# Constants of a 256-step recurrence: from bf16 matmuls to copies into PSUM by ScalarE

## The reference

```
# layer 0: gated recurrence; xz, xr, xh = x @ W_z, W_r, W for all steps; v* = cond @ C* + b*
z = sigmoid(xz[t] + h @ U_z + vz)
r = sigmoid(xr[t] + h @ U_r + vr)
hh = tanh(xh[t] + (r * h) @ U + vh)
h = (1 - z) * h + z * hh
# layer 1: h starts as cond, leak = 1 - alpha
gate = sigmoid(h1 @ Wh.T + x1[t] @ Wz.T + b)
h1 = tanh(h1 * leak + gate * x1[t])
# layer 2: forget and input gates, cumulative products and sums over the steps, started from cond
# layer 3: c = layernorm(cond); hid = gelu(c @ W1 + bias1); w = hid @ W2 + bias2  -> rank 8 factors
#          mid = gelu(x @ base_down + ranks); out = mid @ base_up + ranks
```

## Time and profile before

| | us |
|---|---|
| median of 3 runs (1059.47 to 1060.64) | 1059.53 |
| profiled execution | 1062.49 |
| its span | 1060.7 |

### The profile page before, as it was taken

How to read it: one execution, slowest core, us unless ns; L and a number is a source line. 1 busy time by engine, 2 the same in 40 slices (tenths; PEclk the granted TensorE clock), 3 DMA queues, 4 the chain that set the end, 5 groups by cost and what they waited for, 6 DMA issues and landing times.

```text
span 1060.7 us, 121712 instructions
## 1 busy us (share of the span) xinstructions
PE 988.8 (93%) x55016; PEld 831.4 (78%) x55016; DVE 764.0 (72%) x2501; ACT 507.9 (48%) x2279; POOL 258.3 (24%) x654
## 2 busy tenths in 40 slices
PE   3599999999999999999999999969999999999987
PEld 2599999999999999999999999426566665665655
DVE  2166666666666666666666666699999999999993
ACT  2155555555555555555555555324444444434440
POOL 0022222222222222222222222322322322222220
PEclk9699999999999999999999999989999999999998
DMA  4113303311010010010010010100000100001001
GB/s 168 70 45 112 104 22 114 101 27 30 22 35 22 25 32 22 25 32 25 22 35 22 22 35 22 40 0 23 23 22 22 45 22 22 22 22 40 27 23 40
DMA packets 38292, 42.00 MB, mean 40 GB/s; under 512 B 5120, under 2 KB 31232, under 8 KB 37120
## 3 DMA queue, kind: packets, MB, share of 16 engines
q1 hardware_dynamic: 37408, 41.24, 12.4%
q10 hardware_dynamic: 864, 0.49, 0.2%
HBM read 32.80 MB, written 8.91 MB: 39 GB/s over the span
## 4 chain that ended last, share of the span: by engine, by line
PE 60%; DVE 29%; issue 8%; ACT 1%; DVEq 1%; DMA 1%; ACTq 0%
PE bank L651 31%; PE bank L669 22%; DVE arena L578 10%; DVE wx L590 4%; DVE cx L594 4%; PE bank L661 3%; DVE cx L603 2%; DVE cx L607 2%; DVE wx L576 2%; DVE cx L599 2%; DVE y L618 2%; PE bank L800 1%; PE bank L817 1%; DVE none_h L518 1%; DMA bias<-in_bias 1%
## 5 line engine op out<-in xcount | busy, mean ns | idle before, releaser
L669 PE MATMUL bank<-x_ahead,wx 128*32 128x64 f32 x12384 | 298.6, 222 | 3.3 <-issue 3.3
L661 PE MATMUL bank<-ident,const_stack 96*32 96x64 bf16 x4144 | 251.0, 197 | 6.2 <-issue 4.5
L651 PE MATMUL bank<-none_h,urz 128*32 128x32 f32 x16384 | 215.2, 201 | 20.5 <-DVE none_h L518 13.9
L669 PEld LDWEIGHTS bank<-x_ahead,wx 128*32 128x32 f32 x12384 | 223.9, 111 | 3.7 <-issue 3.7
L651 PEld LDWEIGHTS bank<-none_h,urz 128*32 128x32 f32 x16384 | 188.7, 111 | 33.5 <-DVE none_h L518 27.0
L273 POOL TENSOR_TENSOR leaked<-leak,h_f 128x64 f32<-128x64 f32 x256 | 83.0, 324 | 501.0 <-ACT h_f L366 501.0
L506 DVE TENSOR_TENSOR rh_f<-r_f,none_h 128x32 f32<-128x32 f32 x512 | 104.5, 244 | 136.4 <-ACT r_f L346 136.4
L800 PE MATMUL bank<-x,wl 128*128 (+1 forms) x384 | 179.0, 605 | 0.9 <-DVE rank_rows L555 0.9
L518 DVE TENSOR_TENSOR_SCAN none_h<-zero_z,cand_kept 128x64 f32<-128x64 f32 x512 | 121.5, 279 | 79.8 <-ACT cand_kept L355 79.8
L661 PEld LDWEIGHTS bank<-ident,const_stack 96*32 96x32 bf16 x4144 | 143.3, 97 | 7.0 <-issue 5.2
L366 ACT ACTIVATE h_f<-pre 128x64 f32<-128x64 f32 x256 | 65.9, 257 | 164.0 <-DVE pre L540 164.0
(11 more groups left out here) (81 smaller groups left out, 1387.7 us busy)
## 6 DMA issues: line engine op xcount, KB each, us to landing
x_in<-in_x SPq DMA_DIRECT2D x34, 256.0 KB, 2.7
x_ahead<-in_x SPq DMA_DIRECT2D x130, 64.0 KB, 1.8
arena<-in_w SPq DMA_DIRECT2D x8, 1024.0 KB, 5.5
out<-y SPq DMA_DIRECT2D x32, 256.0 KB, 2.4
rank_rows<-in_bias_rows SPq DMA_DIRECT2D x1, 1024.0 KB, 5.0
arena<-scratch SPq DMA_DIRECT2D x64, 16.0 KB
cx<-in_cx SPq DMA_DIRECT2D x1, 768.0 KB, 4.5
wx<-in_wx SPq DMA_DIRECT2D x1, 768.0 KB, 7.4
```

The lines of the kernel that those rows point to most:

```text
L651: mm = pe.matmul(out(m)[32 * j:32 * j + 32], weights(k, j, m), moving(k), start=False, stop=k == 1, tile_position=(0, 32 * j), skip_group_ ...
L661: pe.matmul(out[32 * j:32 * j + 32], const_stack[:, j, gate * SLAB + m * BLK:gate * SLAB + (m + 1) * BLK], ident[:].rearrange("p v b -> p ...
L669: pe.matmul(out[32 * j:32 * j + 32], weights(k, j, m), moving(k), start=False, stop=False, tile_position=(0, 32 * j), skip_group_check=True)
```

## The change

- ACT copies the constants (as 128x128 float32 pieces, `seed_rh`, `seed_z`, `seed_g`) into the PSUM banks ahead of each block, and the matmuls of `constants` are gone. Two copies stand behind the candidate of each odd step (reset and candidate banks), two behind that of each even step (update bank, layer 1 bank). PE waits for `rh_seeded`, `z_seeded` and `g_seeded`.
- In the opening matmuls with zeros set the banks' state once; the constants are computed transposed, straight in feature order; the bf16 parts, the identity and their stacks are gone. Loads are reordered and spread over SyncE's and ACT's queues.
- The waits at three places are written in the other order.
- SyncE's load of a block's x waits for one count of `r_pre` less (`2 * ((c - 2) * STEPS) + 1` for `2 * (c * STEPS - 3)`; a step gives two counts).
- The adapter's gelu moves from the opening on ACT to behind `second_state` of step 3. Behind the loop the adapter's products and the last two layer 1 gates stand in another order.

```diff
@@ scalar
+            act.wait_ge(bits_set, 1)
+            act.wait_ge(seeds_ready, 8)
+            seed_reset(0)
+            seed_keep(0)
+            seed_reset(1)
+            seed_gate(1)
             act.wait_ge(ln_step, 3)
             act.activation(std[:], var_eps[:], ACT.Sqrt).then_inc(std_done, 1)
-            act.wait_ge(hid_pre, 1)
-            for m in range(HALVES):
-                act.activation(hid_f[:, m], banks[4][:, m * B:(m + 1) * B], ACT.Gelu,
-                               bias=bias1[:, m:m + 1]).then_inc(hid_done, 1)
...
+            def hidden():
+                act.wait_ge(hid_copied, 1)
+                for m in range(HALVES):
+                    act.activation(hid_f[:, m], hid_raw[:, m], ACT.Gelu, bias=bias1[:, m:m + 1]).then_inc(hid_done, 1)
...
                     candidate(n, u)
+                    t = n * BODY + u
+                    if u % STEPS:
+                        seed_reset((u // STEPS) % 2, 2 * t + 2)
+                    else:
+                        if second or u:
+                            act.wait_ge(z_done, 2 * t)
+                        seed_keep(1 - (u // STEPS) % 2)
+                        if second:
+                            act.wait_ge(gate_done, t - LAG + 1)
+                        else:
+                            act.wait_ge(gate_pre, u + 1)
+                        seed_gate(((u - LAG) // STEPS) % 2)
                     if second:
                         second_state(n, u)
+                    if first and u == LAG:
+                        hidden()
@@ vector
                 for m in range(HALVES):
-                    dve.wait_ge(cand_done, 2 * t + m + 2)
                     if m == 0:
                         dve.wait_ge(kept_done, t + 1)
+                    dve.wait_ge(cand_done, 2 * t + m + 2)
@@ tensor
-            def ahead(out, gate, m, weights, moving, start):
-
-                constants(out, gate, m, start)
+            def ahead(out, m, weights, moving):
+
                 for k in range(HALVES):
...
+            def ahead_first(block, par, gate, m):
+
+                if gate == 0:
+                    pe.wait_ge(rh_seeded, 2 * block + m + 1)
+                elif gate == 1 and m == 0:
+                    pe.wait_ge(z_seeded, block + 1)
...
                 def state_ready(k):
-                    pe.wait_ge(h_done, 2 * t + k + 1)
                     if k == 0:
                         pe.wait_ge(cand_done, 2 * t + 1)
+                    pe.wait_ge(h_done, 2 * t + k + 1)
...
                 def reset_ready(k):
-                    pe.wait_ge(rh_done, 2 * t + k + 1)
                     if k == 0:
                         pe.wait_ge(r_done, 2 * t + 2)
+                    pe.wait_ge(rh_done, 2 * t + k + 1)
```

More of the change, by code:

```diff
@@ L198, in next_turn @@
                 for c in range(2, BLOCKS + 2):
-                    sp.wait_ge(r_pre, 2 * (n * BODY + c * STEPS - 3))
+                    sp.wait_ge(r_pre, 2 * (n * BODY + (c - 2) * STEPS) + 1)
                     sp.dma_start(x_ahead[:, c % 2], io["x"][:, bass.ds(n * BODY + c * STEPS, STEPS)]
@@ L451, in _, with repeated, seed @@
         def _(dve):
+            dve.memset(zero_z[:], 0.0).then_inc(zero_done, 1)
+            dve.memset(cand_kept[:], 0.0).then_inc(cand_done, 1)
+            dve.memset(none_h[:, 1], 0.0).then_inc(h_done, 2)
+            dve.memset(x1_f[:], 0.0).then_inc(x1_done, 1)
+            dve.memset(h1_f[:, 0], 0.0)
+            dve.wait_ge(alpha_in, 32)
+            dve.memset(eps[:], EPS).then_inc(eps_done, 1)
+            dve.tensor_scalar(leak[:], leak[:], -1.0, 1.0, ALU.mult, ALU.add).then_inc(leak_done, 1)
+            dve.transpose(bias_f[:].rearrange("p a m b -> p (a m b)"),
+                          bias_rows[:].rearrange("p a e -> p (a e)")).then_inc(bias_done, 1)
+            dve.wait_ge(bias_done, 1)
+            def repeated(out, *parts):
+                return [bass.broadcast_tensor_aps(out, part)[1] for part in parts]
+            for m in range(HALVES):
+                dve.tensor_copy(seed_g[:, m], *repeated(seed_g[:, m], bias_f[:, 3, m:m + 1])).then_inc(seeds_ready, 1)
+            dve.wait_ge(first_in, 16 * len(FIRST_LOADS))
+            dve.wait_ge(const_pre, 1)
+            def seed(out, gate, m):
+                const, bias = repeated(out, pre_const[:, gate, m:m + 1], bias_f[:, gate, m:m + 1])
+                dve.tensor_tensor(out, const, bias, ALU.add).then_inc(seeds_ready, 1)
+            for m in range(HALVES):
+                seed(seed_rh[:, m, 0], 0, m)
+                seed(seed_rh[:, m, 1], 2, m)
+            for m in range(HALVES):
+                seed(seed_z[:, m], 1, m)
             dve.wait_ge(adapter_in, 16 * len(ADAPTER_LOADS))
@@ L493, in _ @@
[L493 to L500 removed]
+            dve.wait_ge(hidden_in, 16 * len(HIDDEN_LOADS))
@@ L656, in recur @@
                 return mm
-            def constants(out, gate, m, start):
-                for j in range(SLABS):
-                    pe.matmul(out[32 * j:32 * j + 32], const_stack[:, j, gate * SLAB + m * BLK:gate * SLAB + (m + 1) * BLK],
-                              ident[:].rearrange("p v b -> p (v b)"), start=start, stop=False,
-                              tile_position=(0, 32 * j), skip_group_check=True)
-            def ahead(out, gate, m, weights, moving, start):
-                constants(out, gate, m, start)
+            def ahead(out, m, weights, moving):
                 for k in range(HALVES):
@@ L746, in second_gate @@
                       lambda k: h1_f[:, (s - 1) % 2, k]).then_inc(gate_pre, 1)
-            for par in range(2):
-                for m in range(HALVES):
-                    constants(pre_g[par][:, m].rearrange("p v b -> p (v b)"), 3, m, start=m == 0)
             FILL = [[(0, 0)], [(0, 1)], [(2, 0)], [(2, 1), (1, 0), (1, 1)]]
```

171 lines of the change are left out of this document (78 added, 93 removed).

## The result

| | before | after |
|---|---|---|
| median of 5 runs each, us | 1060.16 (1059.47 to 1060.64) | 1064.09 (1062.78 to 1066.27) |
| ratio to before, 95% interval | | 1.0042 [1.0026, 1.0059] |
| profiled execution, its span | 1062.49, 1060.7 | 1062.78, 1060.9 |
| four steps in the middle, us | 9.76 | 9.90 |

The change makes the kernel slower by 0.4%. The forecast was 1051. The two profiled executions lie closer together than the medians, because that of before is above its median and that of after is the fastest of its five: 0.3 us apart, the medians 3.9. The difference of 3.6 us is spread between runs.

What follows compares the result with a forecast made beforehand. It took three steps of four to be bound by the cycle PE, ACT, DVE, PE, and one by PE. Terms -6.3, -3.3, +2.9, +1.0, -3.0 and +0.3 sum to -8.4: median 1051.1 us, own range 1045 to 1057, with rivals 1039 to 1059.

Steps and rivals of the forecast that it cites:

- part 5: 60 turns in the loops: constants, PE's and DVE's waits, copies and load sum to -0.05 a turn, -3.0 us.
- Part 1: Opening up to the first product with the state: splitting of constants goes, loop starts at 17.4 for 23.75, -6.3 us.
- Part 2: PE's first turn: fewer matmuls, about one idle piece in seven has nothing to bring in, -3.3 us.
- Parts 3 and 4: Ahead of step 4: gelu's table loads hold up the reset gate, +2.9 us; clock may return late, +1 us.
- Constants: Loop turn: constant matmuls taken off PE, a set taking 0.03; -0.09 ahead of the branch, -0.06 ahead of U's product.
- PE's wait: Loop, three steps of four: the state's wait on a separate instruction delays PE's weights; +0.05 a step, +0.15 a turn.
- Less 0.01 for new register instructions: Loop, ahead of the product with U: new register instructions reduce the constants' gain from -0.06 to -0.05 a turn.
- Part 6: Steps 4 to 15: the scan's well-placed candidate wait is lost, +0.10 in each of three turns, +0.3 us.
- C: Rival: ACT's copies end late and hold up h_f and r_f, +51 us over 256 steps, 1102; chance 0.08.
- B: Rival: the clock stays low behind the gelu, two turns take half as long again, 1059; chance 0.11.
- D: Rival: first turn paced by bringing in instructions, so opening and first turn gain only 3 us together, 1058; chance 0.11.
- A: Rival: the reordered waits do what the change says, -25 us in the loops instead of -3, 1029; chance 0.10.

Runs made afterwards that it cites:

- run 9: The kernel before, with the 1 MB load of rank_rows put last of the tail's five loads; 1060.0 us, ratio 0.9989.
- Run 7: The changed kernel with the adapter's two gelus behind step 5 instead of step 3; 1067.0 us, ratio 1.0051.
- run 2: The changed kernel with PE's wait for the block's x moved from the even steps to the second filling of the step before; 1054.0 us, ratio .9954.
- run 10: The kernel before without its constant matmuls in the recurrence, nothing copied instead, waits kept; 1047.2 us, ratio .9883.
- run 3: The kernel before with only PE's two pairs of waits put in the changed kernel's order; 1075.3 us, ratio 1.0149.
- run 1: The changed kernel with PE's two pairs of waits back in the order of before; 1051.6 us, ratio .9922.
- Run 12: The kernel before with one more, long fulfilled wait on PE ahead of the even steps' filling; 1075.3 us, ratio 1.0145.
- run 5: The changed kernel with PE's old wait order, the wait for x moved a step earlier, and the candidate's wait on the scan; 1024.9 us, ratio .9660.
- run 8: The changed kernel with only the candidate's wait put on the scan itself; 1048.2 us, ratio .9895.
- run 6: The changed kernel with each of ScalarE's copies into PSUM in the recurrence made twice; 1063.7 us, ratio 1.0027.

## Why the prediction was wrong

The step that failed is in part 5: a second wait in PE's queue ahead of the filling, priced at 0.01 us a turn, costs about 0.2. The parts one by one:

- **Part 1, opening, -6.3: right in size** (-6.03; the loop at 17.72 for 17.4), with some luck. It was `bias1`, landing at 15.83, and not the square root's branch that came last (`ada_f` was there at 15.1), and the terms of the forecast add up to a root at 13.7, not 13.9. In the variants of after, with the same opening, the loop starts between 16.3 and 17.7.
- **Part 2, first turn, -3.3: right in size** (-4.07), but not for its reasons. The piece of 4.53 "stays", I wrote. It went, and run 9 puts 0.9 to 1.4 us of it down to the load beside it. "One idle piece in seven" doesn't hold either: each of the 64 matmuls taken out is bf16 and stands once in the trace, a float32 one twice, so with their weight loads the turn has 1536 instructions for 1664, one in thirteen. The single traces scatter by more than that: the first turn takes 22.9 to 24.8 us in after and its variants.
- **Parts 3 and 4, gelu and clock, +3.9: mis-sized** (+0.94, and even that is within the scatter of step 4). My lower bound, "0 if PE is idle just there", was the case; I took "the idle pieces are over then", but the sixth lay at 38.99. Run 7 shows the price without that cover, 3.1 and 0.85. The clock did fall, as part 4 feared, but run 7 has it low there without the gelu, and run 2 doesn't have it low with the gelu.
- **Part 5, -3.0: the step that failed** (+8.1). Its terms, per turn:
  - Constants -0.15 ("a set takes 0.03"): -0.23 by run 10, a set costing 0.04 to 0.05, which is far under the rival price of 0.1.
  - PE's wait +0.15: +0.21 on before (run 3), and taking it out of after gives 0.19 (run 1). The mechanism and the slack of 0.02 were right; the handover costs 0.09 and not 0.07.
  - "Less 0.01 for new register instructions": this is where it broke. I counted the new instructions at next to nothing and gave no reason. It holds for a register instruction without a wait, which runs while products still start; one that carries a wait starts behind the last of them. Run 12 gives +0.21 for such a second wait in the kernel before. In after it is worth 9.897 - 9.308 - 0.186 - 0.209 = 0.19 if the other two waits are right already (runs 5, 1, 8), and 0.08 by itself (run 2): the three edits aren't independent, and why isn't settled.
  - VectorE's wait -0.06, ScalarE's copies 0, SyncE 0: right (0.02 a step; run 6). For SyncE only the trace speaks: PE waits nowhere for the x.
  - Sum -0.23 + 0.21 + 0.20 - 0.06 = +0.12, measured +0.14. The 0.02 left is not settled, and most of the terms are measured on before, not on after.
- **Part 6, +0.3: mis-sized** (+1.0). The same missing term gives 0.2 in each of three turns, and 0.25 is in step 5, which still runs at the low clock (2.59 us, 2.34 in later such steps).
- **Rivals.** C (slower, by the copies) had the right sign by the wrong mechanism: the margin isn't 0.04 us, four copies fit. B fell, the granted clock being back at 0.98 from 46 to 48 us, and D, since 10.1 us were gained by step 4. A named what the waits are worth when they hang rightly, at 1029; run 5, which moves the wait for x as well, measures 1024.9.

The built order showed all three instructions of the failed step, in a row: register, register with the wait for x, product with the wait for the copy. I read their count and not what each can do while it waits.

## What to carry to other kernels

Order the waits ahead of a critical instruction so that the one fulfilled last stays on the instruction itself, and read the built program for it: the same waits in the other order, at two places on PE, cost 15.6 us here. Take fulfilled waits out of an engine's tight stretch, or hang them on instructions that have slack; each cost PE 0.1 us in run 12. A change that takes work off a busy engine shows its gain only when nothing new stands in that engine's queue, so count instructions that do nothing, too.

## What the runs showed of the hardware

- Of two waits directly ahead of an instruction, the first in the program's order stayed on it and the second became a separate instruction ahead; with a register instruction between, the earlier wait went onto that. The Trainium skill ("Perfetto Trace Analysis", Identifying Dependency Chains) knows the separate instruction; which wait it takes, and that it costs 0.09 us on PE and 0.07 to 0.09 on VectorE, is what the runs add.
- ScalarE to VectorE takes 0.03 us with the wait on the scan, 0.10 behind a separate wait, 0.12 behind a register instruction with the wait.
- On PE the weights whose threshold a register instruction works out start 0.084 to 0.088 us after it where nothing else holds them up; behind the register instruction of line 703 in the first step of a turn, which itself takes longer (0.06 in step 100), it is 0.109.
- PE's loop brought in no instructions after its first pass with 1664 (before) and 1536 (after) products and weight loads per pass; with 3072 it did in every pass, and the kernel took almost twice the time.
- The start of step 4 lies between 39.3 and 42.0 us in the traces of after and its variants, with the same opening. What moves it isn't settled; it is some of the spread between runs. One thing that differs is the granted clock: it is 0.50 from 20 to 22 us in all of them, and back at 1.00 from 28 us in run 2, from 36 in after, and only from 44 in run 1.
